# Prefetch hints on the loops of two softmax layers, and TensorE's two transposes moved among the sums

## The chip, the cores and the metric

One Trainium2 chip (trn2); the program runs on one core. The metric is the device time of one execution in microseconds. "Before" is the median of three runs. In the profile PE is TensorE (PEld its weight loads and its sequencer), DVE is VectorE, ACT ScalarE, POOL GpSimd, SP the SyncE queue.

## What is computed

A graph with 6250 nodes of 256 features and 106250 edges sorted by destination goes through two blocks: two graph-convolution layers, then a graph-attention layer with 4 heads and a transformer-style attention layer with one. The part that matters here are the two attention layers, and in both this softmax over the edges of one destination:

```python
def _segment_softmax(logits, seg, n):
    m = jax.lax.stop_gradient(jax.ops.segment_max(logits, seg, num_segments=n))
    e = jnp.exp(logits - m[seg])
    s = jax.ops.segment_sum(e, seg, num_segments=n)
    return e / (s[seg] + 1e-16)
...
logits = jax.nn.leaky_relu(a_src[src] + a_dst[dst], negative_slope=0.2)
alpha = _segment_softmax(logits, dst, n)
msg = h[src] * alpha[:, :, None]
x1 = jax.ops.segment_sum(msg, dst, num_segments=n).reshape(n, H * C1) + gat_bias
```

## The kernel before, in words

**Groups.** The edges are cut into 52 groups (NGW) of 16 columns (UW) of 128. Every layer goes through the groups in order. GpSimd gathers the source rows of a group with 16 indirect DMAs, up to four groups ahead (NBW buffers of G), straight-line code without a loop. The other engines have one program each, tied together by semaphores alone.

**The loops.** In the graph-attention layer (`gat_layer`) and in the transformer layer (`transformer_layer`) the helper `passes` writes a few groups out, then opens a loop on the engine it is called for (L857 and L1440) whose body holds eight groups (NLOOP) and which runs six times, and then writes out what is left. Inside a group's body there are conditional blocks, `pe.If(nwin > 1)`, for groups whose destinations span more than 128 nodes. They are skipped by a taken branch in almost every group. In the graph-attention layer these are L1254 (extra scores) and L1288 (extra sums), the second just ahead of the next group's start or of the loop's closing branch.

**A group k in the graph-attention layer.** VectorE adds the scores and the gathered part into L (L1094), scans it for a running maximum inside the columns (F at L1113, W at L1116, which raises `s_s1`), builds the turned one-hots ohT of group k+1 (L973), and then needs the first and last columns of W turned into rows: it waits for TensorE's transposes (`s_rt`), scans the rows (L1130, L1132), forms In and Out (L1136, L1139, which raises `s_s2`), builds the plain one-hots of group k+1 (L967), and waits for In and Out turned back into columns (`s_bt`, L1153). From these come the maxima M and the difference z; ScalarE takes the exponential (L1362 to L1369); VectorE multiplies the gathered rows by it in four quarters (L1078, Gp, `s_gp`).

**TensorE's order in group k** (`body` in the tensor block): the carry factor psF (L1251), the conditional block L1254, the sums of group k-1 in quarters (`add(q)`: four products of 264 columns each at L1245, the last quarter with the four carry products L1243). The two row transposes (L1270, L1271, behind `s_s1`) stand between the third and the fourth quarter. Then the sixteen score products of group k+1 (L1207, four columns each), then the two transposes back (L1280, L1281, behind `s_s2`), three products of 512 columns whose result nobody reads (L1283, psW), and the finished nodes' transposes and products (`node_turn` L1215, which waits for VectorE's L1040; `node_multiply` L1222, which waits for ScalarE's copy L1325).

**In the transformer layer** scores (L1812) and sums (L1822) alternate column by column, and VectorE's dot products (L1573) follow each score; two score banks are in flight.

Of the kernel before, what the change touches and what calls it, by code (L numbers as in the profile page):

```python
# [40 lines left out]
NGW = NC // UW  # L41
# [3 lines left out]
NLOOP = 8  # L45
# [764 lines left out]
def gat_layer(nc, m):  # L810

    tag = "g3_"
    LD, ST, NQ = 16, 32, UW // QW
    GL = UW * 16
    SW = HC + 1
    with ExitStack() as c:
# [37 lines left out]
        def passes(eng, body):  # L854

            body(0, 0, 0, 0, None)
            with eng.Fori(0, (NGW - 1) // NLOOP) as t:  # L857
                past = None
                for j in range(1, NLOOP + 1):
                    past = body(t * NLOOP + j, t * (NLOOP // NBW) + j // NBW, t * (NLOOP // 2) + j // 2, j % NBW, past)  # L860
            past = None
            for k in range((NGW - 1) // NLOOP * NLOOP + 1, NGW + 1):
                past = body(k, k // NBW, k // 2, k % NBW, past)
# [335 lines left out]
        def _(pe):  # L1199
# [25 lines left out]
            def body(k, kq, kh, b, past):  # L1225
                logits, agg, lead = parts(k)
# [6 lines left out]
                def add(q):  # L1233
                    if q == 0:
                        pe.wait_ge(s_ev, n1 + 1)
                        pe.wait_ge(s_pw, k)
                    pe.wait_ge(s_gp, (k - 1) * NQ + q + 1)
                    hold(m, pe)
                    for u in range(q * QW, q * QW + QW):
                        if u == UW - 1:  # L1240
                            pe.wait_ge(s_scol, k)
                            for h in range(H):
                                nc.tensor.matmul(ps[0:1, h * SW:h * SW + SW], scol[:, h:h + 1], stage[:, h * SW:h * SW + SW],  # L1243
                                                 start=False, stop=False)
                        last = nc.tensor.matmul(ps[:, 0:AGW], oh[:, b1, u, :], Gp[:, b1, u, :], start=(u == 0), stop=(u == UW - 1))  # L1245
                    last.then_inc(s_aq, 1)
# [15 lines left out]
                                last = nc.tensor.matmul(psA[:, u * H:u * H + H], ohT[:, u, :], winx[:], start=True, stop=True)  # L1262
                            last.then_inc(s_xpa, 1)
                if agg:
                    for q in range(3):
                        add(q)
                if logits:
                    pe.wait_ge(s_s1, k + 1)
                    hold(m, pe)
                    nc.tensor.transpose(psR[0:H, 0:P], W[:, :, 0], m.ident[:])  # L1270
                    nc.tensor.transpose(psR[0:H, P:2 * P], W[:, :, UW - 1], m.ident[:]).then_inc(s_rt, 1)  # L1271
                if agg:
                    add(3)
                if lead:
                    for q in range(NQ):
                        score(k + 1, kh + (b % 2), b + 1, q)
                if logits:
                    pe.wait_ge(s_s2, k + 1)
                    hold(m, pe)
                    nc.tensor.transpose(psB[:, 0], In[:], m.ident[0:H, 0:H])  # L1280
                    nc.tensor.transpose(psB[:, 1], Out[:], m.ident[0:H, 0:H]).then_inc(s_bt, 1)  # L1281
                    for j in range(3):
                        nc.tensor.matmul(psW[:], m.ident[:], m.rows[:, 0:2, :], start=True, stop=True)  # L1283
                if agg:
# [113 lines left out]
def transformer_layer(nc, m):  # L1398

    tag = "g4_"  # L1400
    LD, ST, NQ = 32, 16, UW // QW
    GL = QW * 16
    with ExitStack() as c:
# [31 lines left out]
        def passes(eng, body):  # L1435

            past = None, None
            for k in range(3):
                past = past[1], body(k, k // NBW, k // 2, k % NBW, past[0])
            with eng.Fori(0, (NGW - 4) // NLOOP) as t:  # L1440
                past = None, None
                for j in range(3, 3 + NLOOP):
                    past = past[1], body(t * NLOOP + j, t * (NLOOP // NBW) + j // NBW, t * (NLOOP // 2) + j // 2, j % NBW, past[0])
            past = None, None
            for k in range((NGW - 4) // NLOOP * NLOOP + 3, NGW + 2):
                past = past[1], body(k, k // NBW, k // 2, k % NBW, past[0])
# [594 lines left out]
```

## Time and profile before

| | us |
|---|---|
| median of the runs | 4656.9 |
| lowest, highest of the 3 runs | 4648.12, 4657.92 |
| the profiled execution, span from first to last instruction | 4657.7 |
| graph-attention loop, first to last L1094 | about 2329 to 3456 |
| transformer layer, first score to the end | about 3505 to 4657 |

The page gives no other time for the profiled execution than its span. "Busy" counts matmuls, vector and scalar operations and gathers; branches, waits and register operations are the sequencer's and are not counted. Idle time before an instruction is given in square brackets in the timeline with what ended it; "issue" means that the profile shows nothing that it waited for. PEclk is TensorE's granted clock, 1.00 being 2.4 GHz and 0.50 being 1.2 GHz. Each matmul of the program shows as two in the records.

### The profile page before, as it was taken

The numbers are of one execution on the slowest core, as the hardware profiler recorded it, in microseconds if no ns is written. First come the engines' busy times: TensorE is split into PE (matmuls) and PEld (weight loads), VectorE is DVE, ScalarE is ACT, GpSimd is POOL, SyncE is SP. The second block draws the span as 40 slices with busy tenths as digits, with TensorE's granted clock in tenths as the row PEclk, the third lists the DMA queues.
The fourth block names the chain that finished last, engine by engine and source line by source line (L and its number), as shares of the span: only waits on it lengthen the run. The fifth ranks groups of instructions, "written<-read, shape, count | busy, mean of one in ns | idle before, by whom it ended". The sixth has DMA issues, their size and how long they took to land. (4 is left out here: it accounts for less than half of the span.)

```text
span 4657.7 us, 73581 instructions
## 1 busy us (share of the span) xinstructions
PE 3535.7 (76%) x14587; PEld 2519.3 (54%) x14588; DVE 2670.9 (57%) x10225; ACT 741.8 (16%) x2298; POOL 3229.3 (69%) x3404
## 2 busy tenths in 40 slices
PE   2366666666566666666588888988887989999988
PEld 2244444444344444444366666666665766766766
DVE  8544444444333444344377777877776766766765
ACT  3200000000011111111011111111111223222222
POOL 3477777777677777777677776767627777766762
PEclk7687778778798999898878888888888999999999
DMA  5544444444444444444455555555425555555552
GB/s 163 137 130 129 131 131 129 129 131 132 114 138 136 137 136 139 139 138 134 120 149 150 149 147 140 147 140 145 137 73 143 162 152 153 159 143 151 153 145 82
DMA packets 339366, 639.85 MB, mean 137 GB/s; under 512 B 85419, under 2 KB 218598, under 8 KB 338790
## 3 DMA queue, kind: packets, MB, share of 16 engines
q0 software_dynamic: 159744, 440.25, 35.4%
q1 hardware_dynamic: 159993, 180.48, 12.2%
q10 hardware_dynamic: 19056, 12.87, 1.0%
q8 instruction: 189, 3.10, 0.3%
q14 instruction: 384, 3.15, 0.2%
HBM read 569.33 MB, written 63.99 MB: 136 GB/s over the span
## 5 line engine op out<-in xcount | busy, mean ns | idle before, releaser
L582 POOL DMA_INDIRECT g_G<-t,srcI x1664 | 1587.6, 954 | 507.2 <-issue 507.2
L755 PE MATMUL g_ps<-g_G,g_oh 128*128 128x256 f32 x3328 | 1030.9, 460 | 479.6 <-DMA g_G<-t,srcI 392.9
L755 PEld LDWEIGHTS g_ps<-g_G,g_oh 128*128 128x128 f32 x3328 | 725.5, 228 | 749.1 <-issue 418.8
L881 POOL DMA_INDIRECT g_G<-t,srcI x832 | 806.1, 969 | 302.2 <-issue 247.2
L1471 POOL DMA_INDIRECT g_G<-t,srcI x832 | 793.5, 954 | 291.5 <-issue 252.1
L1812 PE MATMUL g_psA<-g_win,g_ohT 128*128 128x257 f32 x1664 | 546.6, 413 | 104.1 <-issue 58.8
L1573 DVE CUSTOM_DVE_ANT_0 g_junk<-g_G,g_psA 128x257 f32<-128x257 f32 x832 | 348.1, 418 | 290.4 <-PE g_psA L1812 265.2
L1822 PE MATMUL g_ps<-g_G,g_oh 128*128 128x257 f32 x1664 | 508.2, 389 | 0.0
L1245 PE MATMUL g_ps<-g_Gp,g_oh 128*128 128x264 f32 x1664 | 451.1, 424 | 47.6 <-issue 26.1
L636 DVE TENSOR_SCALAR g_oh<-iota,g_relx,g_wx 128x128 f32<-128x128 f32 x1664 | 452.1, 364 | 53.3 <-PE g_ps L755 29.4
L1812 PEld LDWEIGHTS g_psA<-g_win,g_ohT 128*128 128x128 f32 x1664 | 293.2, 197 | 211.5 <-issue 84.8
L1245 PEld LDWEIGHTS g_ps<-g_Gp,g_oh 128*128 128x128 f32 x1664 | 334.7, 209 | 116.8 <-issue 51.2
L643 DVE TENSOR_TENSOR g_a<-g_stage,g_own 128x256 f32<-128x256 f32 x106 | 45.7, 431 | 549.2 <-ACT g_stage L800 549.2
L1822 PEld LDWEIGHTS g_ps<-g_G,g_oh 128*128 128x128 f32 x1664 | 318.0, 194 | 67.8 <-issue 23.5
L1915 ACT ACTIVATE g_oh<-g_oh,g_p 128x128 f32<-128x128 f32 x832 | 248.7, 387 | 6.4
L1548 DVE TENSOR_SCALAR g_oh<-iota,g_relx 128x128 f32<-128x128 f32 x832 | 247.0, 299 | 3.1 <-issue 2.8
L1078 DVE TENSOR_TENSOR g_Gp<-g_G,g_psP 128x1024 f32<-128x1024 f32 x208 | 239.5, 1213 | 1.7 <-ACT g_pf L1363 1.7
L1283 PE MATMUL g_psW<-rows,ident 128*128 128x512 f32 x312 | 227.6, 889 | 0.0
L1207 PEld LDWEIGHTS g_psA<-g_win,g_ohT 128*128 128x128 f32 x1664 | 211.6, 207 | 12.7 <-issue 9.5
L1207 PE MATMUL g_psA<-g_win,g_ohT 128*128 128x4 f32 x1664 | 206.7, 261 | 8.6 <-DVE g_ohT L973 8.6
L800 ACT ACTIVATE g_stage<-g_ps 128x256 f32<-128x256 f32 x104 | 39.9, 383 | 1001.6 <-PE g_ps L755 1001.6
L650 DVE SCALAR_TENSOR_TENSOR g_o<-g_psO,g_rec,rows 128x256 f32<-128x256 f32 x106 | 51.3, 484 | 255.1 <-DMA t<-g_t 147.9
(293 smaller groups left out, 3880.3 us busy)
## 6 DMA issues: line engine op xcount, KB each, us to landing
g_G<-t,srcI POOLq DMA_INDIRECT x3328
g_relb<-relrow SPq DMA_DIRECT2D x104, 512.0 KB, 5.6
g_own<-t SPq DMA_DIRECT2D x159, 128.0 KB, 2.2
t<-g_t SPq DMA_DIRECT2D x53, 132.0 KB, 2.7
g_rec<-t SPq DMA_DIRECT2D x53, 132.0 KB
g_rec<-h SPq DMA_DIRECT2D x53, 128.5 KB, 2.6
x<-g_o SPq DMA_DIRECT2D x53, 128.5 KB, 2.8
g_rec<-x SPq DMA_DIRECT2D x53, 128.5 KB, 2.7
```

The lines of the kernel that those rows point to most:

```text
L582: pool.indirect_dma_start(G[:, b, u, :], None, table, IOA(ap=m.srcI[:, g * UW + u:g * UW + u + 1], axis=0)).then_inc(s_g[b][u // QW], 16)
L636: nc.vector.tensor_scalar(oh[:, u, :], m.iota[:], relx[:, u:u + 1], wx[:, u:u + 1], ALU.is_equal, ALU.mult).then_inc(s_oh, 1)
L755: last = nc.tensor.matmul(ps[:, 0:D], oh[:, u, :], G[:, b, u, :], start=(u == 0), stop=(u == UW - 1))
L881: pool.indirect_dma_start(G[:, b, u, :], None, m.t3, IOA(ap=m.srcI[:, g * UW + u:g * UW + u + 1], axis=0)).then_inc(s_g[b], 16)
L1207: last = nc.tensor.matmul(psA[:, u * H:u * H + H], ohT[:, u, :], win[:, b % 2, :], start=True, stop=True)
L1245: last = nc.tensor.matmul(ps[:, 0:AGW], oh[:, b1, u, :], Gp[:, b1, u, :], start=(u == 0), stop=(u == UW - 1))
L1471: pool.indirect_dma_start(G[:, b, u, :], None, m.t4, IOA(ap=m.srcI[:, g * UW + u:g * UW + u + 1], axis=0)).then_inc(s_g[b][u // QW], 16)
L1548: return nc.vector.tensor_scalar(oh[:, b % 4, u, :], m.iota[:], relx[:, b % 2, u:u + 1], None, ALU.is_equal)
L1573: nc.vector.tensor_tensor_reduce(out=junk[:, u % 2, :], in0=G[:, b, u, :], in1=psA[:, u % 2, 0:RW], scale=1.0, scalar=0.0, op0=ALU.mult, o ...
L1812: nc.tensor.matmul(psA[:, u % 2, 0:RW], ohT[:, u, :], win[:, r, :], start=True, stop=True).then_inc(s_pa, 1)
L1822: last = nc.tensor.matmul(ps[:, r, 0:RW], oh[:, b2, u, :], G[:, b2, u, :], start=(u == 0), stop=(u == UW - 1))
L1915: last = nc.scalar.activation(src[:, u, :], src[:, u, :], ACT.Copy, scale=p[:, r, u:u + 1])
```

## The change

In TensorE's body of the graph-attention layer the row transposes move from behind the third quarter of the sums to behind the first, and the transposes back move from behind the next group's scores to ahead of them.

```diff
@@ gat_layer, passes
-            with eng.Fori(0, (NGW - 1) // NLOOP) as t:
+            with nc.Fori(0, (NGW - 1) // NLOOP, engines=bass.OrderedEngineSet([eng.engine]), hint_back_edge=True) as t:
@@ gat_layer, tensor block, body
                 if agg:
-                    for q in range(3):
-                        add(q)
+                    add(0)
                 if logits:
                     pe.wait_ge(s_s1, k + 1)
                     hold(m, pe)
                     nc.tensor.transpose(psR[0:H, 0:P], W[:, :, 0], m.ident[:])
                     nc.tensor.transpose(psR[0:H, P:2 * P], W[:, :, UW - 1], m.ident[:]).then_inc(s_rt, 1)
                 if agg:
-                    add(3)
-                if lead:
-                    for q in range(NQ):
-                        score(k + 1, kh + (b % 2), b + 1, q)
+                    for q in range(1, NQ):
+                        add(q)
                 if logits:
                     pe.wait_ge(s_s2, k + 1)
                     hold(m, pe)
                     nc.tensor.transpose(psB[:, 0], In[:], m.ident[0:H, 0:H])
                     nc.tensor.transpose(psB[:, 1], Out[:], m.ident[0:H, 0:H]).then_inc(s_bt, 1)
+                if lead:
+                    for q in range(NQ):
+                        score(k + 1, kh + (b % 2), b + 1, q)
+                if logits:
                     for j in range(3):
                         nc.tensor.matmul(psW[:], m.ident[:], m.rows[:, 0:2, :], start=True, stop=True)
@@ transformer_layer, passes
-            with eng.Fori(0, (NGW - 4) // NLOOP) as t:
+            with nc.Fori(0, (NGW - 4) // NLOOP, engines=bass.OrderedEngineSet([eng.engine]), hint_back_edge=True) as t:
```

## Rows read from the trace of the kernel before

**Rows 1.** Windows of both layers: length, then busy us (count) of each engine, PEclk, DMA share, GB/s

```profile
2329.00:3475.00 1146.00, 1019.29 (x4713) 738.38 (x4714) 875.25 (x3040) 171.55 (x620) 789.65 (x815) 0.85 0.52 140
3505.00:4657.00 1152.00, 1048.29 (x4539) 775.33 (x4539) 783.43 (x3747) 319.55 (x1042) 790.33 (x829) 0.96 0.52 145
```

**Rows 2.** The branches closing the two loops, by line, TensorE's sequencer: ns min/median/max

```profile
L857 PEldq COMPARE_BRANCH  x6: 76/5050/5251, 2518.4 to 3411.4; - x6
...
L1440 PEldq COMPARE_BRANCH  x6: 76/5346/5740, 3735.9 to 4600.0; - x6
```

**Rows 3.** Timeline of TensorE around a closing branch: start, us, what, idle before

```profile
2518.87 0.70 PE L1223 MATMUL g_psO<-bqk,ones 1*128 1x257 f32 x2
2524.03 0.55 PE L1251 MATMUL g_psR<-g_pf,ones 1*128 1x4 f32 x2 [4.47 <-issue]
2527.94 8.00 PE L1245 MATMUL g_ps<-g_Gp,g_oh 128*128 128x264 f32 x24 [3.36 <-issue]
```

**Rows 4.** Timeline of VectorE in the same group

```profile
2526.68 0.29 DVE L1116 TENSOR_TENSOR_SCAN g_W<-g_mkx,g_F 128x64 f32<-128x64 f32 x1
...
2536.30 0.47 DVE L1130 TENSOR_TENSOR_SCAN g_run<-g_mkr,g_run,g_psR 4x128 f32<-4x128 f32 x1 [6.50 <-issue]
```

**Rows 5.** Windows of single groups, from one L1251 or L1841 to the next

```profile
2524.00:2549.60 25.60, 21.47 (x94) 15.43 (x94) 14.66 (x57) 2.97 (x11) 19.50 (x21) 0.76 0.50 136
...
2594.10:2613.70 19.60, 17.02 (x95) 12.96 (x93) 16.55 (x59) 3.31 (x12) 14.97 (x16) 1.00 0.60 159
2613.70:2638.30 24.60, 21.19 (x94) 15.09 (x93) 17.31 (x61) 3.30 (x12) 18.57 (x20) 0.79 0.57 144
2638.30:2659.50 21.20, 20.34 (x93) 14.77 (x92) 16.64 (x59) 3.31 (x12) 16.33 (x17) 0.84 0.62 155
...
4058.30:4078.80 20.50, 19.67 (x89) 14.45 (x88) 15.06 (x74) 6.10 (x21) 15.03 (x17) 1.00 0.56 155
4078.80:4106.30 27.50, 20.86 (x88) 15.81 (x87) 15.05 (x74) 6.17 (x21) 15.26 (x17) 0.88 0.45 121
```

**Rows 6.** Timeline around a closing branch of the transformer layer, TensorE and VectorE

```profile
4089.33 1.22 PE L1812 MATMUL g_psA<-g_win,g_ohT 128*128 128x257 f32 x2 [6.64 <-issue]
...
4090.59 0.42 DVE L1573 CUSTOM_DVE_ANT_0 g_junk<-g_G,g_psA 128x257 f32<-128x257 f32 x1 [6.62 <-PE g_psA L1812]
```

**Rows 7.** Groups by line and engine, graph-attention layer: busy us, mean ns, idle before

```profile
L1215 PE MATMUL g_psN<-ident,g_t4r 128*128 128x128 f32 x102 | 21.1, 289 | 18.0 <-DVE g_t4r L1040 15.2
L1251 PE MATMUL g_psR<-g_pf,ones 1*128 1x4 f32 x104 | 16.2, 224 | 23.3 <-issue 23.3
...
L1130 DVE TENSOR_TENSOR_SCAN g_run<-g_mkr,g_run,g_psR 4x128 f32<-4x128 f32 x52 | 24.2, 466 | 73.8 <-issue 73.8
```

**Rows 8.** The groups that cost POOL time, page part 5: gathers of both layers

```profile
L881 POOL DMA_INDIRECT g_G<-t,srcI x832 | 806.1, 969 | 302.2 <-issue 247.2 <-DVE g_Gp L1078 54.9
L1471 POOL DMA_INDIRECT g_G<-t,srcI x832 | 793.5, 954 | 291.5 <-issue 252.1 <-PE g_ps L1822 39.2
```

**Rows 9.** The branch that skips the extra scores, L1254, TensorE's sequencer: ns min/median/max

```profile
L1254 PEldq COMPARE_BRANCH  x52: 215/226/3147, 2314.1 to 3453.3; - x52
```

**Rows 10.** Instruction fetches in 2518.9 to 2519.5, then in 2613 to 2616.2: count, MB

```profile
q8 instruction: 2, 0.03, 37.2%
...
q8 instruction: 1, 0.02, 1.8%
```

**Rows 11.** Timelines of two groups: when the sums start, when VectorE scans

```profile
2550.14 5.58 PE L1245 MATMUL g_ps<-g_Gp,g_oh 128*128 128x264 f32 x24 [0.30 <-issue]
...
2551.71 0.27 DVE L1094 TENSOR_TENSOR g_L<-g_G,g_psA 128x64 f32<-128x64 f32 x1
...
2616.00 0.27 DVE L1094 TENSOR_TENSOR g_L<-g_G,g_psA 128x64 f32<-128x64 f32 x1
...
2617.76 0.29 DVE L1116 TENSOR_TENSOR_SCAN g_W<-g_mkx,g_F 128x64 f32<-128x64 f32 x1
```

## The prediction

> **What bounds the kernel now.** I read the windows of the two changed layers first. In the graph-attention layer TensorE is busy for 1019 of 1146 us at a mean clock of 0.85, in the transformer layer for 1048 of 1152 us at 0.96; VectorE has 875 and 783 us, GpSimd 790 in each [rows 1]. So TensorE sets the pace in both, with VectorE close behind in the first. The windows of single groups say the same: a graph-attention group takes 19.6 us when the clock stays at 1.00, 21.2 at a mean of 0.84 and 24.6 in a group that begins with a stall, and TensorE has all but 0.9 to 3.4 us of each; a transformer group takes 20.5 us [rows 5].
>
> GpSimd is the next bound. Its gathers waited for buffers 54.9 us in the one layer (VectorE's Gp) and 39.2 in the other (TensorE's sums) [rows 8]. That is the room in which a faster TensorE can still start gathers earlier; beyond about 55 and 40 us per layer the gathers set the pace.
>
> Then the loops. Each closing branch on TensorE has a minimum of 76 ns, which is the sixth, not taken, and a median of 5.05 us (graph attention) and 5.35 us (transformer) [rows 2]. Five are taken in each layer. The timeline shows what one does: TensorE stands idle for 4.47 us before psF, then 3.36 us more ahead of the sums, and the 24 records of the first three quarters take 8.0 us [rows 3], where a group without a stall needs 5.58 [rows 11]. VectorE finished its scan W at 2526.97 and waits 6.5 us for the row transposes behind those three quarters [rows 4]. In the transformer layer TensorE is idle for 6.64 us and VectorE, which follows it score by score, for 6.62 [rows 6].
>
> **The hints, at their full worth.** Suppose that a hint makes the branch as cheap as the one not taken. In the transformer layer the group with the branch takes 27.5 us and an ordinary one 20.5 [rows 5]: 7.0 us, five times, 35 us. In the graph-attention layer the branch's 5.05 us [rows 2] go, of which the 23.3 us of idle before psF are the visible part (4.66 each) [rows 7], and the group behind it (25.6 us) becomes one like the next-worst, 24.6 [rows 5]: 4.7 + 1.0 = 5.7, five times, 28 us. Together 63 us.
>
> **The hints, at what I expect.** During the branch TensorE's queue of instruction fetches moves two blocks within 0.6 us; a skipped conditional block that stalls has one fetch in its window [rows 10], and the costliest such skip takes 3.15 us [rows 9]. I read the pair as the block behind the loop, which straight-line fetching wanted because the body's last act is to jump over a conditional block (L1288) into the loop's last instructions, and the loop's head, which the branch demanded. The hint can replace the first by the second. But that first request is itself made only on landing behind L1288, right ahead of the branch, so the wait shrinks to that of one fetch and does not vanish: 5.05 - 3.15 = 1.9 us per branch, five times, 9.5 us. In the transformer layer two conditional blocks lie directly ahead of the branch, so the same holds there: 5.35 - 3.15 = 2.2; the other engines must also fetch their loop heads, and VectorE is needed from the third score on, so I take 1.8, five times, 9 us. The ends are 0 (a hint that does nothing) and 63 us. I choose near the lower end because L1254 is the nearest row: the same sequencer, the same kind of branch, one fetch. The added instruction itself is at most 0.1 us on each engine and iteration (the register operations beside it take less than that), under 1 us in all.
>
> The last iteration falls through. If the fetch has been steered to the head, the code behind the loop must then be fetched on demand: up to one 3.15 us [rows 9] per layer, 6 us together; at best nothing. I take 6, since the layer's tail is on the path.
>
> **The row transposes earlier.** This touches no duration. TensorE runs the same instructions; its groups can shorten only by what TensorE waits for VectorE. That is 15.2 us at `node_turn` over the layer [rows 7], some eight groups with 1.8 each. They are the groups that follow a stalled one: VectorE lost its time at L1130, where it waits 73.8 us in total [rows 7], and is late with x1 a group later. With the rows turned behind the first quarter (8 of 24 records, 2.7 of the 8.0 us [rows 3]) VectorE would go on 5 us earlier in such a group, until it meets the plain one-hots, which wait for the later quarters. I count 12 of the 15.2 us. VectorE's 73.8 us are otherwise slack: TensorE is busy meanwhile, so removing that wait gives nothing more. Gathers do not profit directly, as `s_gp` comes from VectorE's Gp.
>
> **The transposes back ahead of the scores.** VectorE waits for them at the end of its one-hots only; that wait is part of the same slack. The scores are needed only at the next L1094, a group's length later. Nothing gained, nothing lost, and the semaphore that frees SP's window load (`s_pa`) comes some 0.3 us later, with two groups in hand.
>
> **Sum.** Against the profiled span of 4657.7: -12 (rows) -9.5 -9 (hints) +6 (fall-through) = -24.5, so 4633; the median of the runs lies 0.8 us below the profiled span, so 4632. A measurement of this kernel tells about 0.2% (9 us) from no change, as its three runs span 9.8 us.
>
> **Rivals.**
> *Full hints.* The steered fetch is made when the sequencer enters the last block in straight line, long ahead of the branch. For it: in the graph-attention layer the code between two skips is long, and the block's border may well lie in it. Against it: both fetches of the pair start only with the branch. Time: 4657.7 - 12 - 63 + 6 = about 4589; with the graph-attention layer alone so, 4615. GpSimd's room (55 and 39 us) allows it.
>
> *Hints that do nothing.* The sequencer fetches in sequence whatever it was told. Then -12 remains, 4646 at best, and 4657 if the wait at `node_turn` only moves to another place. For it: every iteration now pays two fetches for a jump that never changes. The Trainium skill, "Runtime: NRT & Kernel Launch", Instruction fetch mechanics, says that "prefetch is purely sequential" and that a taken branch out of the current window forces a fetch; by that rule this rival is the outcome. The trace agrees with the second half of the rule (5 us where the branch is taken, 76 ns where not) and shows nothing on the first.
>
> *Slower: TensorE waits for W.* Now TensorE needs `s_s1` after four products instead of twelve. In a group at full clock the sums start at 2550.14 and VectorE's L1094 at 2551.71 [rows 11]; W is complete 2.05 us behind L1094 (2616.00 to 2618.05) [rows 11], so at about 2553.8, while a quarter takes a third of 5.58, 1.9 us, and ends at 2552.0. TensorE would stand for 1.8 us in the middle of its sums, in place of the 1.8 at `node_turn`. That is even by itself, and in groups where TensorE is late (sums start 0.6 us behind L1094 as at 2616.6) it does not occur. But idle time lowers the clock: the stalled group has 0.79, and two groups that differ in little else take 19.6 us at 1.00 and 21.2 at 0.84 [rows 5]. If this made some 25 groups, half the layer, into groups of the second kind, it would cost 25 x 1.6 = 40 us against the hints' 12.5 net: 4685; with half as many, 4665. It decides from the point where the first quarter ends more than about 1 us ahead of W in most groups. The Trainium skill, "TensorE: Matmul & The Clock Gate", HAM oscillation, describes the same pattern, a short wait in each round that keeps the engine from staying at 2.4 GHz; by it this rival would be the rule and not the exception. The trace speaks against it so far: the groups with 1.8 us at `node_turn` are the ones at 1.00.
>
> **How the numbers follow.** One fetch saved and rows gained (4632): 0.48. Full hints in one or both layers (4589 to 4615): 0.22. Hints that do nothing (4646 to 4657): 0.14. TensorE waiting for W (4665 to 4685): 0.16. The range holds the first three and the light form of the fourth: 4585 to 4664. Faster by over 0.2% (below 4648): the first two and a small part of the third, 0.71. Within 0.2%: 0.14. Slower by over 0.2%: the rest of the fourth, 0.15.
>
> **What would show it.** The closing branches L857 and L1440 on TensorE at about 3 us instead of 5 (5 again: no hint; below 1: full), and one fetch in place of two there. L1130's idle time on VectorE falls from 73.8 to under 15 us, part of it found again at L967. `node_turn`'s wait for L1040 falls below 4 us. New idle time at L1270 on TensorE, released by L1116, under 20 us; over 40 with a mean clock under 0.83 would be the slower rival. L1254's stalls stay. Wrong altogether would be a change of the graph-attention layer by over 30 us with the closing branches still at 5 us.

## The result, and the profile after

The changed kernel takes 4607.3 us (median of four runs, 4603.1 to 4612.3); the kernel before took 4652.5 beside it (four runs, 4634.7 to 4657.9). The ratio is 0.9899, with a 95% interval of 0.988 to 0.9919. Forecast was 4632: the direction and the range held, the gain came out at nearly twice the forecast. The profiled executions went from 4657.7 to 4609.2, 48.5 us, against 24.5 forecast.

First the windows of both layers in the changed kernel (they answer to [rows 1]), then those of single groups: an ordinary graph-attention group and the one behind a closing branch, and the same two of the transformer layer [rows 5].

```profile
2331.00:3419.00 1088.00, 990.42 (x4707) 709.16 (x4708) 872.12 (x3029) 170.92 (x616) 790.20 (x815) 0.89 0.55 147
3451.00:4609.00 1158.00, 1051.54 (x4539) 775.83 (x4539) 782.13 (x3749) 319.65 (x1042) 796.08 (x830) 0.96 0.52 144
...
2626.40:2646.70 20.30, 18.81 (x93) 13.34 (x93) 16.91 (x60) 3.31 (x12) 15.43 (x17) 0.92 0.58 154
2685.60:2709.30 23.70, 20.25 (x94) 14.89 (x94) 19.29 (x62) 3.35 (x12) 18.11 (x19) 0.86 0.56 150
...
3982.10:4002.60 20.50, 19.46 (x88) 14.44 (x87) 14.82 (x74) 6.14 (x21) 15.36 (x17) 1.00 0.56 157
4023.10:4049.50 26.40, 21.82 (x89) 16.38 (x88) 15.07 (x73) 6.15 (x21) 17.94 (x19) 0.87 0.51 137
```

The graph-attention layer went from 1146 to 1088 us, 58 less. The transformer layer went from 1152 to 1158: it is *longer*, although its group with the closing branch fell from 27.5 to 26.4. So the gain is all in one layer, and the other gives a little back. (Outside these windows the profiled execution is 3.5 us longer than before.)

The branches, by line, TensorE's sequencer (to [rows 2] and [rows 9]):

```profile
L857 PEldq COMPARE_BRANCH  x6: 85/344/361, 2517.0 to 3353.3; - x6
...
L1254 PEldq COMPARE_BRANCH  x52: 221/231/2346, 2316.5 to 3400.1; - x52
...
L1441 PEldq COMPARE_BRANCH  x6: 85/3527/3942, 3681.1 to 4547.6; - x6
```

The closing branch of the graph-attention loop fell from 5.05 to 0.34 us, the other only from 5.35 to 3.53.

The groups by line: waits of VectorE and TensorE in the graph-attention layer and the gathers of both layers (to [rows 7] and [rows 8]).

```profile
L1130 DVE TENSOR_TENSOR_SCAN g_run<-g_mkr,g_run,g_psR 4x128 f32<-4x128 f32 x52 | 24.1, 464 | 6.8 <-issue 6.8
L1153 DVE TENSOR_TENSOR g_T<-mkFL,g_psR 128x128 f32<-128x128 f32 x52 | 14.4, 277 | 4.1 <-PE g_psR L1278 4.1
...
L1251 PE MATMUL g_psR<-g_pf,ones 1*128 1x4 f32 x104 | 15.1, 213 | 0.1
L1269 PE MATMUL g_psR<-ident,g_W 128*4 128x128 f32 x52 | 14.7, 282 | 47.0 <-DVE g_W L1116 47.0
...
L881 POOL DMA_INDIRECT g_G<-t,srcI x832 | 806.7, 970 | 253.3 <-issue 251.5 <-DVE g_Gp L1078 1.8
L1472 POOL DMA_INDIRECT g_G<-t,srcI x832 | 798.5, 960 | 287.7 <-issue 253.3 <-PE g_ps L1823 34.2
```

Three things stand here. VectorE's wait for the row transposes (L1130) fell from 73.8 to 6.8. TensorE has a new wait for W at L1269, 47.0 us, three times its 15.8 before. And the gathers of the layer no longer wait for buffers: their idle time on Gp fell from 54.9 to 1.8 us. 806.7 + 253.3 = 1060 us for 52 groups is 20.4 a group, which is the ordinary group's 20.3. GpSimd now sets the pace of this layer, and while it does a shorter group on TensorE gains nothing.

One row of the kernel before the prediction did not weigh: VectorE's wait for the transposes back, same view.

```profile
L1153 DVE TENSOR_TENSOR g_T<-mkFL,g_psR 128x128 f32<-128x128 f32 x52 | 15.0, 288 | 37.9 <-PE g_psR L1281 37.3 <-issue 0.5
```

Another thing fell with it. TensorE's branches of over a microsecond, at L1254 and L857 together, take 62.2 us in the kernel before (14 skips with 36.8, five closing branches with 25.4) and 9.8 us in the changed one (five skips, and none at L857). Which of the two counts for more is the question of the experiments.

### The profile page after: what moved, and what is told of

It reads as the page before. It is cut to its first block and busy times, and to the rows that moved or that the text cites. A ratio compares the mean times of both kernels' runs of the same rounds, so it can differ in the third digit from the quotient of the medians.

```text
span 4609.2 us, 73629 instructions
## 1 busy us (share of the span) xinstructions
PE 3524.1 (76%) x14587; PEld 2499.9 (54%) x14588; DVE 2667.7 (58%) x10225; ACT 742.4 (16%) x2298; POOL 3235.1 (70%) x3404
## 5 line engine op out<-in xcount | busy, mean ns | idle before, releaser
L1472 POOL DMA_INDIRECT g_G<-t,srcI x832 | 798.5, 960 | 287.7 <-issue 253.3
L881 POOL DMA_INDIRECT g_G<-t,srcI x832 | 806.7, 970 | 253.3 <-issue 251.5
L1245 PE MATMUL g_ps<-g_Gp,g_oh 128*128 128x264 f32 x1664 | 420.5, 403 | 22.3 <-issue 19.2
L1245 PEld LDWEIGHTS g_ps<-g_Gp,g_oh 128*128 128x128 f32 x1664 | 313.2, 196 | 81.9 <-issue 24.1
```

Of the source, the lines that this page charges most:

```text
L881: pool.indirect_dma_start(G[:, b, u, :], None, m.t3, IOA(ap=m.srcI[:, g * UW + u:g * UW + u + 1], axis=0)).then_inc(s_g[b], 16)
L1472: pool.indirect_dma_start(G[:, b, u, :], None, m.t4, IOA(ap=m.srcI[:, g * UW + u:g * UW + u + 1], axis=0)).then_inc(s_g[b][u // QW], 16)
```

## The experiments

Each is given with its ratio to the kernel before on the same chip; 0.0022 of ratio is about 10 us. Kernels that ran on different chips are compared by their ratios, since the median of the kernel before lies between 4651 and 4659 beside them. Theories A and B are defined anew in each text.

### Hints and order apart

`hints_only` is the kernel before with both hints; `order_only` has TensorE's new order and plain loops.

```diff
 hints_only
-            with eng.Fori(0, (NGW - 1) // NLOOP) as t:
+            with nc.Fori(0, (NGW - 1) // NLOOP, engines=..., hint_back_edge=True) as t:
-            with eng.Fori(0, (NGW - 4) // NLOOP) as t:
+            with nc.Fori(0, (NGW - 4) // NLOOP, engines=..., hint_back_edge=True) as t:
```

> The hints in both layers, TensorE's order as before. Theory A (the hint in the graph-attention layer is the gain: the branch 5.05 to 0.34 us, five times, with what follows it, and the skip stalls at L1254 that went with it): most of the 45 us come, about 4617 us (graph-attention layer 40 us shorter, L1254's stalls under 12 us as in the changed kernel). Theory B (the order of TensorE's work carries half or more): the branch is short just the same, but VectorE's wait at L1130 stays over 50 us and the time is 4630 or more. Transformer layer: 1115 us between its first and last score product on VectorE, as in the changed kernel, where it was 1109.4 before, if the hint there is what costs.

> TensorE's new order, loops without hints. Theory A: 12 us or less, 4641 or more, closing branches at 5 us. Theory B: 20 us or more, 4630 or less, L1130's wait under 15 us. The slower rival of the prediction, TensorE waiting for W at L1269 and a lower clock: slower than before, clock under 0.83 in the graph-attention layer. If the L1254 stalls (14 with 36.8 us before, 5 with 9.8 us after) hang on the order of the instructions and not on the hint, they are fewer here too.

The two hints together gave nothing: 4660.0 against 4659.0, ratio 1.001 (0.9999 to 1.0022). The order alone gave 32 us: 4627.2, ratio 0.993 (0.991 to 0.995). Theory A (the hint is the gain) fell. The closing branch in each, `hints_only` first:

```profile
L857 PEldq COMPARE_BRANCH  x6: 85/3222/4104, 2516.1 to 3403.7; - x6
```

```profile
L857 PEldq COMPARE_BRANCH  x6: 76/4061/4228, 2515.6 to 3379.2; - x6
```

In the old order the hint shortens the branch to 3.2 us, the prediction's 3.15 nearly to the digit, and it is worth little (how much is seen below, where the transformer hint, which costs, is left out). The new order without the hint has 4.1 us. Only hint and new order together give 0.34.

The two single hints, on both sides:

```diff
 gat_hint_order: the changed kernel, and
-            with nc.Fori(0, (NGW - 4) // NLOOP, engines=..., hint_back_edge=True) as t:
+            with eng.Fori(0, (NGW - 4) // NLOOP) as t:
 tf_hint_only: the kernel before, and
-            with eng.Fori(0, (NGW - 4) // NLOOP) as t:
+            with nc.Fori(0, (NGW - 4) // NLOOP, engines=..., hint_back_edge=True) as t:
```

> The changed kernel without the hint in the transformer layer. If that hint is worth its 1.8 us at each of five branches, the time is 9 us above the changed kernel, 4616. If it is the hint that made the layer 5.6 us longer between first and last score product, the time is 5 us below it, 4602, and the layer is back at 1109 us. If the layer is longer because of where its gathers stand after a faster first layer, this run keeps the longer ordinary groups (20.4 to 20.5 us against 20.1 to 20.2) and gains nothing.

> The kernel before with the hint in the transformer layer alone. If the hint itself makes ordinary groups there 0.3 us longer: the time is the kernel before's plus 5, and groups at 20.4 to 20.5 us. If the longer groups come from the layer ahead having ended sooner: ordinary groups at 20.1 to 20.2 us, closing branches at 3.1 to 3.9 us, the time 5 to 9 us below before.

`gat_hint_order`: 4598.1, ratio 0.9874 (0.9857 to 0.989). So with the order in place the graph-attention hint is worth another 29 us over 4627.2 (a repeat, below, has the ratio 0.9893, which makes it 17), and the transformer hint *costs*: by the ratios 3 to 12 us, with intervals that overlap. `tf_hint_only` says the same from the other side, with an interval that leaves out 1: 4662.5, 1.0015 (1.0002 to 1.0028), 7 us. By the same count the graph-attention hint in the old order is worth only the 2.5 us between `tf_hint_only` and `hints_only`, less than these two can tell from nothing.

### The two pairs of transposes apart

```diff
 rows_hint: gat_hint_order, and
-                [transposes back]
                 [scores of group k+1]
+                [transposes back]
 back_hint: gat_hint_order, and
-                    add(0)
+                    for q in range(3):
+                        add(q)
                 [row transposes]
-                    for q in range(1, NQ):
-                        add(q)
+                    add(3)
 back_only: back_hint, and the graph-attention loop
+            with eng.Fori(0, (NGW - 1) // NLOOP) as t:
```

> Graph-attention hint kept, no transformer hint; only the row transposes moved, the transposes back behind the scores as before. To be read against 4598 us with both moved. Theory A (it is the wait for s_s2 standing between the scores and psW that leaves borders without a fetch, so the back transposes' place counts): closing branch at 3 to 4 us, L1254 stalls at several groups, 4630 or more. Theory B (the rows' place is the gain): L1130's idle time under 15 us, 4600 to 4615, closing branch at 0.34.

> The other half: only the transposes back moved ahead of the scores, row transposes behind the third quarter as before, graph-attention hint kept, no transformer hint. Theory A: closing branch at 0.34 us, L1254 stalls five times only, VectorE's wait at L1130 above 50 us all the same, 4600 to 4620. Theory B: hardly better than the hints in the old order, 4640 or more.

> Only the transposes back moved ahead of the scores; rows as before, no hint anywhere. So far: nothing 4659, both moved 4627, both moved with the graph-attention hint 4598, back moved with that hint 4601, rows moved with that hint 4734. Theory A (the back transposes' place is the whole gain of the order, since VectorE's wait for them at L1153, 35 us before, stands ahead of M, z, the exponential and Gp): 4625 to 4640, L1153's wait under 5 us. Theory B (the rows' place carries a part wherever the closing branch still stalls): above 4640, with L1130's wait over 60 us.

| | without hint | graph-attention hint |
|---|---|---|
| neither moved | 1 | about 1 (`hints_only` 1.001, with the transformer hint as well) |
| rows moved | not run | 1.0175 (1.0158 to 1.0192), 4734.1 |
| back moved | 0.992 (0.9892 to 0.9949), 4617.0 | 0.9889 (0.9872 to 0.9906), 4601.4 |
| both | 0.993 (0.991 to 0.995), 4627.2 | 0.9874 and 0.9893, 4598.1 and 4602.9 |

The move on which the forecast put 12 us costs 82 us when made alone; the one that it priced at nothing carries the gain, 41 us by itself by the medians (37 by the ratio). With the back transposes moved, moving the rows as well gives nothing (4601 against 4598 and 4603). Without a hint it gives nothing either: 0.993 against 0.992, two intervals that overlap almost wholly.

`back_only`, groups by line, where L1130's wait stays at 51.5 and does not matter, and then its branches:

```profile
L1130 DVE TENSOR_TENSOR_SCAN g_run<-g_mkr,g_run,g_psR 4x128 f32<-4x128 f32 x52 | 24.3, 468 | 51.5 <-issue 51.4
L1153 DVE TENSOR_TENSOR g_T<-mkFL,g_psR 128x128 f32<-128x128 f32 x52 | 14.3, 275 | 0.7 <-PE g_psR L1278 0.7
...
L881 POOL DMA_INDIRECT g_G<-t,srcI x832 | 805.4, 968 | 255.4 <-issue 250.9 <-DVE g_Gp L1078 4.5
...
L857 PEldq COMPARE_BRANCH  x6: 76/3683/4232, 2509.8 to 3364.3; - x6
...
L1254 PEldq COMPARE_BRANCH  x52: 208/226/3066, 2313.5 to 3405.9; - x52
```

L1153's 37.9 us are gone and with them 50 of the 54.9 us that the gathers waited for Gp. But the long branches of TensorE went from 62.2 to 33.5 us in the same step, and it is they that explain most of it. The layer from its first to its last L1094, and the time of the branches over a microsecond (L1254 and L857), in the profiled execution of each:

| | layer, us | long branches, us | L1153's wait, us |
|---|---|---|---|
| kernel before | 1126.9 | 62.2 | 37.9 |
| `hints_only` | 1123.5 | 56.4 | 29.1 |
| `tf_hint_only` (this layer as before) | 1109.7 | 47.6 | 33.0 |
| `gat_hint_moved` (below) | 1105.5 | 45.0 | 29.5 |
| `order_only` | 1089.1 | 35.2 | 4.1 |
| `second_wait` (below) | 1091.9 | 35.1 | 4.1 |
| `back_only` | 1078.0 | 33.5 | 0.7 |
| changed kernel | 1068.9 | 9.8 | 4.1 |
| `gat_hint_order` | 1060.5 | 10.2 | 4.1 |

The code of this layer is the same in `tf_hint_only` as before, so the long branches differ between executions too. Among the first four, all with the transposes back in their old place, a microsecond of long branches goes with about 1.2 us of layer; `gat_hint_order` and `second_wait`, both with the new place, differ by 24.9 us of branches and 31 us of layer, which is the same rate. By it the 28.7 us of branches that `back_only` is rid of are some 36 of the 48.9 us by which its layer is shorter. Carried on to 34 us of branches, the old place would have some 1092 us of layer, where the three kernels of the new place have 1078 to 1092: an estimate of 0 to 14 us for L1153's wait and all else, from single executions. So the gain of the order is in the main the shorter branches. No run moves L1153's wait without them.

The cost of the rows moved alone is another thing. `rows_hint` has only 26.9 us of long branches and is the slowest of all. Its timelines show what the place of these two tiny transposes can do. TensorE:

```profile
2594.03 0.27 PE L1269 MATMUL g_psR<-ident,g_W 128*4 128x128 f32 x1 [2.10 <-DVE g_W L1116]
...
2600.35 3.91 PE L1207 MATMUL g_psA<-g_win,g_ohT 128*128 128x4 f32 x32
2604.19 0.26 PE L1280 MATMUL g_psR<-ident,g_In 4*128 4x4 f32 x1
2604.32 0.24 PE L1281 MATMUL g_psR<-ident,g_Out 4*128 4x4 f32 x1
```

and VectorE, the same group:

```profile
2593.60 0.29 DVE L1116 TENSOR_TENSOR_SCAN g_W<-g_mkx,g_F 128x64 f32<-128x64 f32 x1
...
2604.81 0.29 DVE L1153 TENSOR_TENSOR g_T<-mkFL,g_psR 128x128 f32<-128x128 f32 x1 [2.81 <-PE g_psR L1281]
...
2609.47 4.60 DVE L1078 TENSOR_TENSOR g_Gp<-g_G,g_psP 128x1024 f32<-128x1024 f32 x4
2614.00 0.27 DVE L1094 TENSOR_TENSOR g_L<-g_G,g_psA 128x64 f32<-128x64 f32 x1
```

This is a ring, and both engines wait in it. W ends at 2593.89 and TensorE turns the rows at 2594.03. Then it has three quarters of the sums and sixteen scores in its queue before it turns In and Out back, until 2604.56: 10.5 us. VectorE stands 2.8 us for that, starts L1153 at 2604.81, and needs 9.2 us for M, z, the exponential on ScalarE and Gp until the next L1094 at 2614.00. From L1094 to the end of W it is 2.3 us (2591.62 to 2593.89 in this group), then TensorE, which has stood 2.1 us for W, goes on. 10.5 + 0.3 + 9.2 + 2.4 = 22.4 us a round, where the gathers need 20.4. Over the layer L1153 waits 148.6 us and L1269 103.6. The 10.5 us are an ordinary case: the median of the 52 groups is 10.7.

In the kernel before, with one quarter and the scores between the pairs, the median distance is 6.6 us, a round of 18.5 by the same sum; a group whose scores took 5.0 us in place of 3.6 has 8.0 (2504.18 to 2512.2) and 19.9. In the changed kernel TensorE goes from L1269 at 2692.13 to the end of L1278 at 2698.82, 6.7 us, a round of 18.6. Both lie below a group, so the ring did not set the pace of the kernel before, and the gain is not a shorter ring; in `back_only` the distance is down to 3.1 us. L1153's 37.9 us are 0.7 us a group: VectorE has some 6 us of its own between the two hand-overs and waits for the rest of the 6.6. Rows early and back late lengthens the ring, and that costs once the round is longer than a group.

### What makes the closing branch cheap

In the changed kernel, `gat_hint_order` and `back_hint` L857 takes 0.34 us; in `hints_only` and `rows_hint`, which share the old place of the transposes back, 3.2 and 3.0. Three kernels ask why.

```diff
 gat_hint_moved: the kernel before, and
+            with nc.Fori(0, (NGW - 1) // NLOOP, ..., hint_back_edge=True, head_slot={TensorE: 197}) as t:
+            with nc.Fori(0, (NGW - 4) // NLOOP, ..., hint_back_edge=False, head_slot={TensorE: 108}) as t:
 second_wait: gat_hint_order, and behind the scores of group k+1
+                if logits:
+                    pe.wait_ge(s_s2, k + 1)
+                    hold(m, pe)
 wait_beside: gat_hint_order, and the same two lines ahead of the first wait for s_s2
```

> TensorE's old order, hint in the graph-attention layer alone, and TensorE's loop there begun 20 instructions earlier against the borders of the fetched blocks, so that the last border in the loop falls behind the wait for s_s2 and not ahead of it. In the old order four to five of twelve borders were passed without a fetch following (the fetch came only with the next skip or the closing branch, which then stalled), in the new order none. Theory A (it is where the borders fall against the waits in the body): the closing branch takes 0.34 us as in the changed kernel, and the time is 20 us or more below before. Theory B (it is the order of the work itself, wherever the borders are): the branch stays at 3 to 4 us as with hints in the old order, L1254 still stalls ten times or more, and the time is within 8 us of before.

> Both moved, graph-attention hint, no transformer hint, and a second wait for s_s2 (long fulfilled, one instruction) between the scores and psW, where the old order had it. Theory A (a wait instruction at that place of the code makes TensorE's queue pass a border without a fetch): L1254 stalls at ten groups or more, closing branch at 3 to 4 us, 4620 or more. Theory B (it is when the queue really stands and moves on, and not the instruction): 5 stalls, closing branch 0.34, 4598 within 5 us.

> Control for second_wait (4638): the same extra wait for s_s2, the same number of instructions, but right beside the first one, ahead of the transposes back, so that nothing waits between the scores and psW. Theory A (the wait's place between scores and psW makes the queue stall): 4598 within 6 us, closing branch 0.34, L1254 stalls five times. Theory B (one more instruction in every group moves all borders, and that alone did it): 4620 to 4640, closing branch at 3 to 4 us.

`gat_hint_moved`: 4641.8, 0.998 (0.9968 to 0.9993), the five taken closing branches 3.0 to 4.2 us: not the place in the blocks, or not that alone. (Its row at L857 counts seven branches; the one of 0.41 us at 2340.7 leads into the loop.) It is also the only kernel with the graph-attention hint alone in the old order: 9 us, if the new places that it gives both loops (`head_slot`) bring nothing by themselves. `second_wait`: 4638.1, 0.9957 (0.9944 to 0.9971). `wait_beside`: 4602.0, 0.9894 (0.987 to 0.9919). The rows of `second_wait`, and those of `wait_beside`:

```profile
L857 PEldq COMPARE_BRANCH  x6: 85/3044/3844, 2512.4 to 3375.4; - x6
...
L1254 PEldq COMPARE_BRANCH  x52: 220/233/2644, 2312.8 to 3419.6; - x52
```

```profile
L857 PEldq COMPARE_BRANCH  x6: 85/346/431, 2517.5 to 3353.9; - x6
...
L1254 PEldq COMPARE_BRANCH  x52: 222/231/2572, 2318.6 to 3398.3; - x52
```

The same wait, long fulfilled, costs nothing beside its twin and about 30 us between the scores and psW (0.9957 against 0.9894; the medians, from two chips, lie 36 apart). There the closing branch goes back from 0.34 to 3.0 us although the hint is executed as before, and eight skips at L1254 stall for over a microsecond instead of five. The trace's instruction fetches (q8) show the difference: in the changed kernel, `order_only`, `back_hint` and `wait_beside` TensorE's queue asks for its last block 5.6 to 9.3 us ahead of each taken closing branch, while the scores run (in the changed kernel at 2508.0 for the branch at 2517.0); in the kernel before, `hints_only`, `rows_hint` and `second_wait` the last request is 18 to 23 us ahead (2498.2 for the branch at 2518.4), in one of the twenty 0.3. During the branch itself the kernel before makes two requests, `hints_only`, `second_wait` and `order_only` one, the changed kernel none: 5.05 us, 3.0 to 4.1 us, 0.34 us. So what the new order does is to have one request made early, and what the hint does, as the rows read, is to make it the right one. That a wait at this place suppresses the early fetch is shown; by what mechanism is not.

```diff
 pe_hint: gat_hint_order, and
+            ..., hint_back_edge=eng is nc.tensor
```

> New order, the graph-attention layer's hint on TensorE alone, no transformer hint. Against 4598 us with it on four engines and 4627 with none. If TensorE's closing branch is what counts: 4600 or below (VectorE's skips cheaper, its 3.4 us behind its branch covered by TensorE's lead). If the others' loop heads count as well: VectorE's 3.4 and ScalarE's 2.8 us stay on the path, 4605 to 4612.

4602.4, 0.9883 (0.9863 to 0.9904). The hints on VectorE, ScalarE and SP add nothing that can be measured here.

### Why the hint costs in the transformer layer

```diff
 tf_dve_nohint: the changed kernel, transformer loop
+            ..., hint_back_edge=eng is not nc.vector
 tf_dve_extra: the changed kernel, transformer loop
+            ..., hint_back_edge=False) as t:
+                if eng is nc.vector:
+                    hold(m, eng)
 tf_slot215: the changed kernel, transformer loop
+            ..., hint_back_edge=True, head_slot={TensorE: 215}
 tf_late: the changed kernel, that loop written by hand
+                    if j == 2 + NLOOP:
+                        armed = eng.mark_branch_hint_location()
...
+                eng.br_lt(...).branch_hint(armed)
 tf_late2: tf_late, and hold(m, eng) before and behind the mark
```

> The changed kernel with the transformer layer's hint on TensorE, ScalarE and SP, and none on VectorE. With a hint, VectorE's skips of conditional blocks took 0.41 and 0.63 us where they took 0.20 and 0.52 without. Theory A (this is what makes an ordinary group 20.45 instead of 20.15 us): ordinary groups back at 20.15, VectorE back at 4.5 us behind its closing branch so that these groups stay at 28 us, the time within 4 us of the kernel without that hint (4598). Theory B (TensorE's hint is what slows): groups at 20.45 and 4607 us or more.

> The changed kernel without the transformer layer's hint, but with one harmless semaphore instruction as the first of VectorE's loop, in the hint's place. Theory A (the hint itself makes the skips dearer): skips at 0.20 and 0.52 us, groups at 20.15, 4598 us. Theory B (one more instruction moves VectorE's code against the borders of fetched blocks, and that is all): skips at 0.41 and 0.63 us, groups at 20.45, 4610 us or more.

> The changed kernel with TensorE's loop of the transformer layer begun at another place against the borders of the fetched blocks, so that the last border before the closing branch is passed in straight line, ahead of the two skipped conditional blocks. Theory A (the hint can act only from such a border on): L1441 on TensorE at 0.1 to 0.4 us, the groups with the branch 2 us shorter (then VectorE's 2.0 us and ScalarE's 2.8 us behind their own branches decide), time 8 to 12 us below the changed kernel. Theory B: the branch stays at 3.1 to 3.9 us and the time at 4607.

> The changed kernel with the transformer layer's hints executed at the start of the last of the eight groups of an iteration, and not at its head. Theory A (each skip that an engine takes while its hint is outstanding costs it 0.1 to 0.2 us more): VectorE's skips at 0.20 and 0.52 us in seven groups of eight and dearer only in the eighth, ordinary groups back at 20.15 us, closing branches as in the changed kernel; 5 to 12 us below the changed kernel, 4595 to 4602. Theory B (the extra time hangs on the loop as a whole): skips at 0.41 and 0.63 in all groups and 4607.

> As tf_late, whose hints did not show up in its trace (no hint was executed in that loop, so it was a repeat of the kernel without the transformer hint: 4603); here with one semaphore instruction before and one behind the hint, at the start of the iteration's last group. Theory A (a skip costs more only while the hint is outstanding): ordinary groups at 20.15 us and VectorE's skips at 0.20 and 0.52 us but in the last group; closing branches as in the changed kernel (TensorE 3.1 to 3.9, VectorE 2.0 us); 4592 to 4600. Theory B (hint too late or tied to the loop): branches 5 us, or skips dear everywhere, 4600 to 4607.

VectorE's skip of a conditional block, by line, first in the kernel before, then in the changed kernel, `tf_dve_extra` and `tf_late2` (ns min/median/max):

```profile
L1634 DVEq COMPARE_BRANCH  x52: 56/56/56, 3568.8 to 4641.9; - x52
```

```profile
L1635 DVEq COMPARE_BRANCH  x52: 56/116/135, 3515.3 to 4594.0; - x52
```

```profile
L1637 DVEq COMPARE_BRANCH  x52: 56/56/56, 3520.4 to 4591.7; - x52
```

```profile
L1648 DVEq COMPARE_BRANCH  x52: 56/56/122, 3511.0 to 4575.5; - x52
```

With the hint every skip takes twice as long, and with what follows it the next instruction starts 0.1 to 0.2 us later. One more instruction in the hint's place does nothing of the kind, so it is not a shift of the code. With the hint executed only ahead of the eighth group, only the skips of that group are dearer. VectorE's chain sets the pace in this layer (scores and dot products take turns), so two skips make an ordinary group 20.45 us instead of 20.15. The window of such a group in `gat_hint_order`, against 20.50 in the changed kernel above:

```profile
3972.90:3993.00 20.10, 19.45 (x88) 14.46 (x87) 14.98 (x73) 6.09 (x21) 15.08 (x17) 1.00 0.58 160
```

0.3 us in some 40 groups are 12 us, and behind the last iteration, whose branch falls through, two groups take 21.5 and 17.4 us where they took 20.2 and 14.2; 3.6 of these 4.5 us are left at the end of the kernel. Against these stand the five groups with a taken closing branch, which fell from 26.4 to 24.3 us in the mean (from the first dot product of one group to that of the next), 11 us. 12 + 3.6 - 11 is about the layer's +6. The same two groups take 20.6 and 14.2 us in `tf_dve_nohint`, so the cost behind the loop hangs on VectorE's hint too.

The times: `tf_dve_nohint` 4595.2, 0.9875 (0.9858 to 0.9891), ordinary groups back at 20.1; `tf_dve_extra` 4603.6, 0.9895 (0.9879 to 0.9912); `tf_late` 4602.9, 0.9893 (0.9876 to 0.991), in whose trace no hint was executed in that loop, so that it is a repeat of `gat_hint_order`; `tf_late2` 4601.1, 0.9888 (0.9858 to 0.9919), skips cheap and branches short (VectorE 2.0 us, TensorE 3.7). All four lie within what repeats of one kernel differ by, so a late hint is no worse than none and not measurably better. `tf_slot215` missed: TensorE's branch stayed at 3.4 us and the kernel took 4620.5, 0.9941 (0.9924 to 0.9957), 13 us more than the changed kernel by the medians and 20 by the ratios. Its profiled execution is the fastest of the four and as long as the changed kernel's (4609.8 and 4609.2), with a transformer layer 8 us longer; why the kernel is slower stays open.

### Fewer closing branches

```diff
 tf_16: gat_hint_order, transformer loop
+            NLT = 16
-            with eng.Fori(0, (NGW - 4) // NLOOP) as t:
+            with eng.Fori(0, (NGW - 4) // NLT) as t:
-                for j in range(3, 3 + NLOOP):
+                for j in range(3, 3 + NLT):
```

> The changed kernel without the transformer hint and with sixteen groups in that loop's body: two taken closing branches instead of five. A group with a closing branch takes 28 us against 20.15, so three fewer should give 3 x 7.9 = 24 us: 4575. If instruction fetches of a body twice as long stall elsewhere, or the gathers take over as the bound (they need 20.3 us a group, 1058 for the layer, where it took 1083): 4585 to 4595.

4585.3, 0.9846 (0.9819 to 0.9872): by the ratios 13 to 22 us below the two runs of `gat_hint_order`, where 24 were expected. The branches and the gathers show where the rest is:

```profile
L1442 PEldq COMPARE_BRANCH  x3: 76/5202/5861, 3853.3 to 4530.8; - x3
...
L1473 POOL DMA_INDIRECT g_G<-t,srcI x832 | 797.2, 958 | 265.1 <-issue 253.1 <-PE g_ps L1824 11.8
```

Two branches are taken instead of five, and the gathers wait 11.8 us for buffers where they waited 39.2 before [rows 8]. What was left of GpSimd's room is nearly used up here as well.

## Why the prediction was half right

- **Bound and room: right** for the graph-attention layer. TensorE set the pace, GpSimd was next, with 55 us of room [rows 8]. The layer gained 58, and its gathers now wait 1.8 us. In the transformer layer VectorE is on the path as well: 0.3 us more on its skips lengthen every group.
- **"The transposes back ahead of the scores... Nothing gained, nothing lost": the step that failed**, together with "L1254's stalls stay". Moved alone they are worth 37 to 41 us (`back_only`). The larger part comes by TensorE's branches, which the sum held fixed but for the hints: with the wait for `s_s2` gone from between the scores and psW, 14 skips of over a microsecond with 36.8 us became 5 with 14.4, and the closing branches fell from 5.05 to 3.7 us without any hint. The smaller part, 0 to 14 us by the estimate above, is left for L1153's wait. The text called that wait "part of the same slack" as L1130's without a row for it; it is 37.9 us and stands directly ahead of M, z, the exponential and Gp.
- **"The row transposes earlier", 12 us: wrong.** Its signs came true, L1130's wait fell to 6.8 us and `node_turn`'s to 3.9 in the layer's window, and gave nothing with the transposes back moved (0.993 against 0.992, 4598 and 4603 against 4601). Alone the move costs 82 us, by a ring that the prediction did not close: it asked who waits for the rows, not what TensorE has to do between them and the transposes back.
- **The slower rival** (TensorE waits for W) has its mechanism in the trace, 47.0 us at L1269 against under 20 forecast, and is still not what decides. It was said to cost through the clock; the granted clock rose from 0.85 to 0.89. The Trainium skill, "TensorE: Matmul & The Clock Gate", HAM oscillation, has waits in every round hold the clock down, in a kernel that waits some 3 to 5 us for a DMA each time. The waits here are far shorter: an ordinary group with 0.7 us of it has 0.92. So this case does not test that section, and to say that "by it this rival would be the rule" went further than it does. Nor is the higher clock the gain: `back_hint` has as short a layer (1069.0 us from its first to its last L1094, 1068.9 in the changed kernel) at 0.86. In `rows_hint` the window's clock was 0.85 as before, and the loss was waiting time.
- **"The hints, at what I expect", 1.9 us per branch in graph attention: right for the old order, wrong for the new.** `hints_only` shows 3.2 us and one request in place of two, as written. That this is worth only some 2 to 9 us there fits the forecast of 9.5 at best; not foreseen was that it goes to 0.34 with the transposes back moved, which brings 14 to 29 us (0.992 to 0.9889, 4627 to 4598). The forecast treated hint and order as terms to be added. The rival "full hints" in this layer alone had 4615, nearest to the outcome, and its mechanism, a steered fetch made in straight line long ahead of the branch, is what the fetches show. What it did not name is the condition, that nothing waits between the scores and psW; and its sum still held the rows' 12 us.
- **"L1254's stalls stay": wrong.** The kernel before has 14 stalls of over a microsecond with 36.8 us in all, the changed one 5 with 9.8. `order_only` has 5 as well (14.7 us), so their number is the order's doing and not the hint's.
- **The transformer hint, -9: mis-signed by a missing term.** The branch fell by 1.8 us as written (5.35 to 3.53), and the groups that hold it by 2.2, but 0.3 us in every group had no place in the sum. The fall-through was priced at 3 us a layer and measured 3.6 in this one.
- **The rival "hints that do nothing"** is near in time for the hints in the old order (`hints_only` 1.001), though not by its mechanism. It rested on the Trainium skill, "Runtime: NRT & Kernel Launch", Instruction fetch mechanics, by which the fetch goes on in sequence only. The trace speaks against that: a hinted branch of 0.34 us, with no fetch during it, leads back to the head of a loop that lies eight groups behind, where the unhinted branch made two requests and took 5.05.
- The sign came out right, and the size at half, partly by luck: a rows term that is nothing and a transformer hint of the wrong sign stood in for the 37 to 41 us that had no term.

## What to carry to other kernels

Before putting a gain down to a wait that vanished, look at what else vanished in the same run. Here the long branches on TensorE's sequencer, which no busy time shows, went with the layer's length at about 1.2 us a microsecond, and moving one wait by sixteen small products changed them. When a transpose or another small step of a serial chain sits in the queue of a busy engine, add up the whole round: from the first hand-over through everything queued behind it to the second, and on to the next group. It costs what the round exceeds the group by. A hint for a loop's branch is to be tested per engine and per loop: it can do next to nothing until a wait ahead of the branch is moved, and it taxes every skip in the body while it stands. And ask which engine is next: here a layer stopped at its gathers, and the rest had to come from the other one.

## What the runs showed of the hardware that was not expected

- A prefetch hint brought a loop-closing branch on TensorE from 5.05 to 0.34 us, but only in the kernels where nothing waited between the scores and psW; one fulfilled wait there in each group brought back 3.0 us and cost about 30 us of 4602.
- While a hint is outstanding, VectorE's skips of a conditional block take 0.116 instead of 0.056 us in the records, and 0.1 to 0.2 us more until the next instruction.
- Where VectorE had the hint, leaving the transformer loop cost 4.5 us in the two groups behind it; where it alone had none (`tf_dve_nohint`) it cost 0.4.
- Still open: why a wait at that one place keeps TensorE's queue from asking for the next block, and why another place of the transformer loop in the blocks (`tf_slot215`) cost 13 to 20 us; and how much L1153's wait is worth by itself.
